# An attention layer with a rotation: sums of the partial contexts moved to the final stage, and the mask penalty of the last 192 key columns moved to TensorE

## What is computed

```
emb = silu(sin_emb(timestep)) @ W_ada + b_ada; scale, shift = split(emb)
x = ln(src) * (1 + scale) + shift
q, k, v = heads(x @ Wq + bq), heads(x @ Wk + bk), heads(x @ Wv + bv)
scores = q @ k.T / sqrt(32) + attention_bias          # the bias is B x 16 x 2048 x 2048 f32, 537 MB
scores = where(mask, -inf, scores)                    # one mask for all heads
ctx = merge_heads(softmax(scores) @ v)
x = x + (ctx @ Wo + bo); h = ln(x) * g2 + beta2
x = x + gelu2(h @ W1 + b1) @ W2 + b2
out = rotation by theta and phi of each four neighbouring columns of x
```

## Time and profile before

| | before |
|---|---|
| median of 3 runs | 3860.55 us |
| the profiled execution, its own time | 3858.61 us |
| its span, first to last instruction | 3857.0 us |
| attention stage, first bias load to last store | 510 to 2719 us |
| final stage | 2719 to 3857 us |
| granted TensorE clock, mean | 0.965 |

### The profile page before, as it was taken

One profiled execution on the slowest core, in us unless ns is written; L12 is line 12 of the kernel. 1 busy time (PEld: TensorE's weight loads), 2 busy tenths in 40 slices (PEclk: granted clock), 3 DMA queues, 4 the chain that ended last, 5 costly groups with the idle time before them and its releaser, 6 DMA issues. The chain is left out here.

```text
span 3857.0 us, 64984 instructions
## 1 busy us (share of the span) xinstructions
PE 3589.8 (93%) x18848; PEld 2074.9 (54%) x18848; DVE 2561.2 (66%) x4882; ACT 1899.6 (49%) x2483; POOL 2165.7 (56%) x595
## 2 busy tenths in 40 slices
PE   6778769999999999999999999999699999999997
PEld 2334336666666666666666666666344444444443
DVE  3444449999989999899999899999322323232232
ACT  1221227777777777777777777777211111111110
POOL 0000059999989999999999999999000000000000
PEclk8889879999999999999999999999799999999999
DMA  5556489999999999999999999997511101101000
GB/s 188 169 173 201 147 288 319 315 313 312 319 348 317 316 312 312 337 331 313 317 315 313 341 319 314 317 313 271 155 22 33 22 11 33 22 22 22 11 11 11
DMA packets 327444, 822.20 MB, mean 213 GB/s; under 512 B 165376, under 2 KB 181760, under 8 KB 250624
## 3 DMA queue, kind: packets, MB, share of 16 engines
q1 hardware_dynamic: 277376, 746.44, 57.6%
q10 hardware_dynamic: 45312, 58.74, 5.6%
q0 software_dynamic: 4736, 16.78, 1.2%
HBM read 737.95 MB, written 83.89 MB: 213 GB/s over the span
## 5 line engine op out<-in xcount | busy, mean ns | idle before, releaser
L450 POOL TENSOR_TENSOR ring<-ring,penb 128x2048 f32<-128x2048 f32 x512 | 2089.4, 4119 | 599.6 <-DMA penb<-pen_scratch 542.5
L555 ACT ACTIVATE ring<-ring,neg_max 128x2048 f32<-128x2048 f32 x512 | 1029.1, 2010 | 515.4 <-DVE neg_max L520 515.4
L618 PEld LDWEIGHTS b_T<-ident,ring 128*128 128x128 f32 x8192 | 886.7, 141 | 623.5 <-ACT probT L564 427.6
L618 PE MATMUL b_T<-ident,ring 128*128 128x128 f32 x8192 | 1158.7, 281 | 1.9 <-DVE probT L492 1.3
L492 DVE COPY probT<-b_T 128x512 f32<-128x512 f32 x1024 | 668.0, 684 | 70.5 <-PE b_T L618 70.5
L506 DVE CUSTOM_DVE_ANT_0 ring<-scores,ring,max_part 128x1024 f32<-128x1024 f32 x512 | 657.6, 1284 | 74.2
L506 DVE CUSTOM_DVE_ANT_0 ring<-scores,ring 128x1024 f32<-128x1024 f32 x512 | 622.2, 1215 | 43.6 <-PE scores L601 43.6
L601 PE MATMUL scores<-keys,queries 128*128 (+1 forms) x2048 | 606.5, 418 | 46.6 <-DMA queries<-q_parts 45.4
L781 POOL TENSOR_TENSOR y_out<-rot_a,rot_b 128x512 f32<-128x512 f32 x32 | 50.3, 1572 | 1020.8 <-DVE rot_b L890 1020.0
L564 ACT COPY probT<-b_T 128x512 f32<-128x512 f32 x1024 | 542.8, 580 | 30.2 <-PE b_T L618 24.0
L634 PE MATMUL bank_ctx<-probT,values 128*32 128x512 f32 x4096 | 546.8, 607 | 0.0
(11 more groups left out here) (91 smaller groups left out, 1926.1 us busy)
## 6 DMA issues: line engine op xcount, KB each, us to landing
ring<-in_fside_Bx16xSxS SPq DMA_DIRECT2D x512, 1024.0 KB, 5.8
keys<-k_parts SPq DMA_DIRECT2D x256, 256.0 KB, 6.8
values<-v_heads ACTq DMA_DIRECT2D x128, 256.0 KB, 6.0
queries<-q_parts SPq DMA_DIRECT2D x512, 64.0 KB, 6.8
pen_scratch<-pen SPq DMA_DIRECT2D x8, 2048.0 KB, 7.2
penb<-pen_scratch SPq DMA_DIRECT2D x32, 512.0 KB, 12.3
xin<-in_x ACTq DMA_DIRECT2D x8, 1024.0 KB, 5.2
mask_in<-in_mask_Bx1xSxS_bk ACTq DMA_DIRECT2D x8, 1024.0 KB, 7.3
```

What stands on the lines that cost most here:

```text
L450: nc.gpsimd.tensor_tensor(ring[:, j, :], ring[:, j, :], penb[:, j, :], ALU.add).then_inc(masked, 1)
L555: nc.scalar.activation(ring[:, k, :], ring[:, k, :], ACT.Exp, bias=neg_max[:, k:k + 1], accum_out=sums[:, k:k + 1]).then_inc(exp_done, 1)
L618: last = nc.tensor.transpose(bankT[n % 2][:, c * P:(c + 1) * P], ring[:, slot, at:at + P], ident[:])
```

## The change

In the attention stage `close`, `sel4`, `bank_sum`, the reciprocal and the scaling go. The four partial contexts are copied (L571 as before) and stored unsummed: 256 KB for 4 tiles in place of 64 KB. The freed PSUM bank becomes a third transpose bank. GpSimd adds the penalty to columns 0 to 1855 only; for the last 192 TensorE adds a matmul of a bf16 identity with `penb` to the last score matmul's bank. VectorE computes the negated sum with a running minimum, so the separate negation L520 goes, and it places one `copy_quarter` behind each `add` (quarter 3 with a lag of three tiles). TensorE's waits stand one or two matmuls ahead of where they are needed. ScalarE keeps row sums and minima of all trips in SBUF and copies the 8 minima once in a trip.

In the final stage SyncE loads the partial contexts, 4 x 256 KB for each block of four heads (c = 0 to 3 of a unit), into two buffers. GpSimd sums them with two additions (of 1024 and 512 columns); TensorE transposes the broadcast reciprocals in place of the context; VectorE multiplies the two. All other fronts are one f later. The rotations of unit u-1 (`late`) are spread over f = 0 to 3 of unit u, behind `hidden`. W1 and W2 are loaded by ScalarE's queue, Wo after the first two context blocks.

```diff
 # phase_b, GpSimd and TensorE
-  nc.gpsimd.tensor_tensor(ring[:, j, :], ring[:, j, :], penb[:, j, :], ALU.add)
+  nc.gpsimd.tensor_tensor(ring[:, j, 0:POOL_MASKED], ring[:, j, 0:POOL_MASKED], penb[:, j, 0:POOL_MASKED], ALU.add)
+                if live(i, NT):
+                    if c == CH - 1:
+                        pe.wait_ge(pen_in[j], (it // H) * 16 + 16)
+                        last = nc.tensor.matmul(scores[c][:, CW - PE_MASKED:CW], identb[:], penb[:, j, POOL_MASKED:S],
+                                                start=False, stop=True)
+            def free_before_turn(it, j, c):
+                t = it * R + j - 2
+                if live(t, NT):
+                    if c == 0:
+                        pe.wait_ge(exp_done, t + 1)
+                    else:
+                        need(pe, out_dve, t * 2 - 1)
-                if j % QT == 2:
-                    close(it, j)
 # phase_b, VectorE
                 add(it, j, 0)
+                copy_quarter(it, j, 3, 3)
                 add(it, j, 1)
-                    nc.vector.tensor_scalar(neg_max[:, j:j + 1], max_part[:, j, CH - 1:CH], -2.0, 0.5, ALU.mult, ALU.mult)
-                copy_quarter(it, j, 2)
-                copy_quarter(it, j, 3)
+                copy_quarter(it, j, 2, 2)
 # phase_b, ScalarE
-                      ctx_out[:, hh, :, :].rearrange("p t d -> p (t d)")).then_inc(ctx_stored[hh], 16)
+                                  ctxp[:]).then_inc(ctx_stored, 16)
 # phase_c, SyncE
+                for c in range(DB):
+                    if isinstance(v, int) and c == 2:
+                        load_vectors()
+                    need(sp, ctxT_ready, v * DB + c - 1)
+                    for k in range(4):
+                        sp.dma_start(parts[DH * k:DH * (k + 1), c % 2, :, :],
+                                     ctx_scratch[bass.ds(v * H + 4 * c + k, 1)].rearrange("o (g d) q -> d (o g) q", d=DH)).then_inc(part_ld[c % 2], 16)
 # phase_c, GpSimd
+            def add_parts(v, c):
+                pool.wait_ge(part_ld[c % 2], v * 128 + (c // 2) * 64 + 64)
+                nc.gpsimd.tensor_tensor(parts[:, c % 2, 0:2, :], parts[:, c % 2, 0:2, :], parts[:, c % 2, 2:4, :], ALU.add).then_inc(halved, 1)
+                pool.wait_ge(halved, added_by_pool(v, c))
+                nc.gpsimd.tensor_tensor(parts[:, c % 2, 0, :], parts[:, c % 2, 0, :], parts[:, c % 2, 1, :], ALU.add).then_inc(summed, 1)
+            def between(v):
+                add_parts(v, 0)
+                add_parts(v, 1)
+                finish(v - 2, 0)
+                finish(v - 2, 1)
+                add_parts(v, 2)
+                finish(v - 2, 2)
+                add_parts(v, 3)
+                finish(v - 2, 3)
 # phase_c, the order of VectorE
             with eng.Fori(1, NU - 1) as u:
                 for f in range(FB + 2):
                     ffn(u, f)
+                    front(u + 1, f)
+                    late(u - 1, f)
```

More of the change, by code:

```diff
@@ L439, in _ @@
                         load_head(b, pair, h, False)
-            for i in range(2):
-                sp.wait_ge(ctx_stored[i], 16 + TRIPS * 16)
+            sp.wait_ge(ctx_stored, UNITS * 16 + 16)
         @block.gpsimd
@@ L621, in weigh @@
-            def weigh(it, j):
-                n = (j - 2) % QT
-                unit = it * 2 - 2 if j < 2 else it * 2 - 1 if j < 6 else it * 2
-                hh = 1 if 2 <= j < 6 else 0
-                if live(unit, UNITS):
-                    if n == 0:
-                        pe.wait_ge(v_in[hh], it * 16 if j == 2 else it * 16 + 16)
-                        need(pe, ctx_copied, unit)
-                    pe.wait_ge(out_act if n < 2 else out_dve, (unit * QT + QT - 1) * 2 + n % 2 + 1)
-                    for c in range(4):
+                if n == 2 and live(t, NT):
+                    need(pe, out_dve, t * 2)
@@ new lines, in turn @@
+                for c in range(QR):
+                    if c == 2:
+                        if n == 0 and live(t, NT):
+                            need(pe, out_act, t * 2)
+                        if n == 1:
+                            copied_before_weigh(it, j)
+                        if n == 2 and live(t, NT):
+                            pe.wait_ge(out_act, t * 2 + 1)
+                    if live(t, NT):
+                        at = (QR * n + c) * P
+                        last = nc.tensor.transpose(turn_bank(slot, n)[:, c * P:(c + 1) * P], ring[:, slot, at:at + P], ident[:])
@@ new lines, in turn, with weighed, copied_before_weigh @@
+                if live(t, NT):
+                    last.then_inc(turned, 1)
+            def weighed(it, j):
+                unit = it * 2 - 2 if j < 2 else it * 2 - 1 if j < 6 else it * 2
+                return (j - 2) % QT, unit, 1 if 2 <= j < 6 else 0
+            def copied_before_weigh(it, j):
+                n, unit, hh = weighed(it, j)
+                if live(unit, UNITS):
+                    pe.wait_ge(out_act if n < 2 else out_dve, (unit * QT + QT - 1) * 2 + n % 2 + 1)
+            def weigh(it, j):
+                n, unit, hh = weighed(it, j)
+                if live(unit, UNITS) and n == 0:
+                    pe.wait_ge(v_in[hh], it * 16 if j == 2 else it * 16 + 16)
+                    need(pe, ctx_copied, unit)
+                for c in range(4):
+                    if live(unit, UNITS):
@@ L634, in weigh @@
                         last = nc.tensor.matmul(bank_ctx[DH * c:DH * (c + 1), :], values[:, hh, QR * n + c, :],
                                                 probT[:, hh, QR * n + c, :], start=(n == 0), stop=(n == 3))
-                    if n == 3:
-                        last.then_inc(pv_done, 1)
-            def close(it, j):
-                unit = closing(it, j)
-                if live(unit, UNITS):
-                    pe.wait_ge(ctx_copied, unit + 1)
-                    pe.wait_ge(ctx_normed, unit + 1)
-                    for t in range(QT):
-                        last = nc.tensor.matmul(bank_sum[:, t * DH:(t + 1) * DH], ctxp[:, t * P:(t + 1) * P], sel4[:],
-                                                start=True, stop=True)
-                    last.then_inc(ctx_summed, 1)
+                if live(unit, UNITS) and n == 3:
+                    last.then_inc(pv_done, 1)
@@ L703, in phase_c @@
         consts_ready = sem("consts_ready")
-        ctx_ld, xm_ld = sem("ctx_ld"), sem("xm_ld")
-        ctx_turned = sem("ctx_turned")
+        part_ld, xm_ld = [sem(f"part_ld{i}") for i in range(2)], sem("xm_ld")
+        halved = sem("halved")
+        summed = sem("summed")
+        first_summed = sem("first_summed")
+        recip_ready = sem("recip_ready")
+        wide_ready = sem("wide_ready")
+        recip_turned = sem("recip_turned")
         ctxT_ready = sem("ctxT_ready")
@@ new lines, in finish @@
+            def finish(u, t):
+                pool.wait_ge(rotated, u * QT + t + 1)
+                need(pool, y_stored[t % 2], u * 32 + (t // 2) * 16)
+                nc.gpsimd.tensor_tensor(y_out[:, t % 2, :], rot_a[:, t % 2, :], rot_b[:, t % 2, :], ALU.add).then_inc(y_ready, 1)
+                pool.wait_ge(y_ready, u * QT + t + 3)
+                pool.dma_start(out[bass.ds(u, 1), t * P:(t + 1) * P, :].rearrange("o p n -> (o p) n"),
+                               y_out[:, t % 2, :]).then_inc(y_stored[t % 2], 16)
@@ new lines, in _ @@
+            add_parts(0, 0)
+            add_parts(0, 2)
+            for c in range(DB):
+                add_parts(1, c)
+            def between(v):
[7 more added lines that the diff above has]
+                finish(v - 2, 3)
+            between(2)
+            with pool.Fori(3, NU) as v:
+                between(v)
@@ L789, in _ @@
+            for u in (NU - 2, NU - 1):
+                for t in range(QT):
+                    finish(u, t)
             for i in range(2):
```

339 lines of the change are left out of this document (170 added, 169 removed).

## The result

The changed kernel takes 3949.84 us (median of four executions, 3944.27 to 3977.22; a fifth took 3931.72) against 3860.34 for the kernel before: ratio 1.0234, 95% interval 1.0182 to 1.0286. A gain to 3680 was forecast; it is a loss of 2.3%. The profiled execution is the longest of its runs, 3977.22 us with a span of 3975.4.

The account below looks back on a forecast made before the run. TensorE and VectorE, tied together, were taken to set the 33.65 us trip, with GpSimd and DMA close behind, DMA becoming first limit. 3857 - 133 (attention) - 45 (final stage) = 3679 us of span, given as 3680; forecast 3640 to 3730, range 3590 to 3775.

Parts of the forecast that it names:

- a store is issued one step earlier: Attention, ScalarE: the earlier store is covered by its slack, busy 25.8 of 33.65 us; uncovered, 0.3 us a trip.
- if the new copy of the context costs the queues more than its bytes: Stated condition for being wrong: the larger context copy costs the DMA queues more than its bytes; no size given.
- SyncE's wait for the slot has room: Attention, bias tile loads: 8 slots of 3.9 us against some 20 us for a tile's load through transposes.
- The DMA term: Attention: 11.28 MB a trip takes 30.7 to 32.9 us; with 0.8 for lockstep, 31.5, saving 133 us.
- GpSimd 3.74: Attention: GpSimd's penalty addition over 1856 of 2048 columns falls from 4.108 to 3.74 us a tile.
- The mask matmul: Attention, TensorE: the new 192-column mask matmul costs 0.11 us a tile, between 0 and 0.25.
- TensorE's tile: Attention: 3.5 to 4.05 us, taken as 3.75, or 30.0 a trip; earlier waits could remove gaps between groups.
- The stall at the change of unit: Final stage: spreading the rotations removes TensorE's 8.4 us stall, 0.5 left for safety, saving 55 us over seven changes.
- GpSimd's sums: Final stage: summing partial contexts takes 15 to 30 us of a 127 us unit, hidden in pauses.
- The start: Start of the final stage, 55.0 us before: 10 us longer from the added loads, between -5 and +20.
- (d): Rival: waits for transfers lower TensorE's clock to a mean of 0.84; trip 35.7 us, about 3943 us; chance 0.06.
- (b): Rival: DMA keeps today's busy rate or TensorE its gaps; trip 32.4 to 32.9 us, about 3753 us; chance 0.22.

Follow-up runs that it names:

- e17: The changed kernel with ScalarE's store of the context issued one step later, where it stood before the change; 3766.1 us.
- e1: The changed kernel with SyncE issuing the query loads one tile earlier in its queue; 3831.1 us.
- e11: The changed kernel with the query loads issued from ScalarE's queue instead of SyncE's; 3873.7 us.
- e6: e1 without the low-by-low product of q and k: three key loads instead of four, six query loads instead of eight; 3714.7 us.
- e16: The changed kernel with the first 512 columns of a tile's scores matmul done twice, slowing TensorE; 3918.2 us.
- e9: e1 with e5's single values load, e6's three key parts, and W1 and W2 loads issued behind unit 0's four reciprocal copies; 3700.9 us.
- e12: The changed kernel with ScalarE issuing the W1 and W2 loads behind unit 0's four reciprocal copies, not ahead of them; 3930.0 us.
- e5: e1 with a head's values loaded once in a trip and the second buffer copied by ScalarE; 3803.6 us.
- e7: e1 with keys loaded only for the first head of each group of 16, wrong keys for the rest, timing only; 3701.2 us.

## Why the prediction was wrong, step by step

**The failed step** is the one on ScalarE's store: "a store is issued one step earlier", costed by ScalarE's own time and covered by its slack. No run showed a cost of it on ScalarE; the cost lay in what the store meets in the DMA engines. e17 puts it at 184 us, more than the whole distance between the changed kernel and the kernel before: with that one issue moved back the kernel takes 3766 us and is a gain again. Of the conditions for being wrong one named it, "if the new copy of the context costs the queues more than its bytes", but no rival carried it.

**"SyncE's wait for the slot has room"** held for the bias tiles as far as it matters (GpSimd waits 222.5 us for them in after, but VectorE for GpSimd only 4.9) and was not asked of the queries, the load with the least room in the same queue: 11.7 us before (issued 1338.06, wanted 1349.74) and 10.8 now. e1 and e11 show that much of the loss passes through here (119 and 76 us back).

**The DMA term.** The bytes were right: e17 moves 342 GB/s at a share of 0.99, and 33.0 x 342 is 11.3 MB, forecast 11.28. The rate was not: 368 GB/s was taken from stretches in which penalty tiles, large loads over all partitions, filled the queue. Between 1200 and 1600 us the best of all runs is 341 and 342, in e6 and e17, just under the 343 from which the upper end, 32.9 us a trip, was worked out. So with the store in its old place a trip is 33.0, not 31.5. The 358 GB/s of the Trainium skill (DMA: Bandwidth & Descriptors, Specifications) was not reached in these windows either.

**The engines.** GpSimd 3.74: right. The mask matmul 0.10 for 0.11: right. TensorE's tile 3.94 for 3.75: the waits set earlier took nothing out of the gaps between the groups: scores 1.02, mask 0.10, turn 0.96, weigh 1.00 and turn 0.85 make 3.93. By that alone the trip could not come under 31.5, the very time that was forecast with 0.8 us of loss already in it.

**The final stage.** The stall at the change of unit is gone, as said; 1.7 us of 8.4 are left, most of it in ScalarE's reciprocal copies (TensorE waits 1.28 us for one, at 2952.94), against 0.5 taken: 7 x 6.7 = 47 us gained for 55. GpSimd's sums hide. The start was mis-sized, +31 for +10: the forecast counted bytes on two queues, but not that ScalarE is held while it issues 8 MB. -47 and +31 are the -16 measured.

**The rivals.** (d) gave the side and nearly the number, 3943, but by luck: it needed a mean clock of 0.84, and measured were 0.94 to 0.96. The clock fell after TensorE's waits for queries and explains one slow tile of 5.4 us a trip (5.43 - 3.94 = 1.5 us); the waits themselves, 131.6 us in 1500, weigh more, some 3.2 us a trip. (b), 3753 with transfers at today's rate, is close to what e17 gives, 3766, and for the reason that it named.

**What stays open.** Why the keys' trough is so much worse when the large store goes ahead of them is seen in the slices and not taken apart; why more TensorE work (e16) gives 32 us back is not explained by it; the small store at the old step of the changed kernel, which would isolate the step, has not been run, nor has e9 with the store at its old step.

## What to carry to other kernels

Moving a DMA's issue is a change to every transfer in flight with it: cost it by what it is now beside, and look at the rate in slices of 1 us at that place, not only at the issuing engine's time. In a queue shared by loads of different urgency, compute the room of the one with the shortest, for it waits behind all the others. And take the rate of a full queue from a stretch with the same mix of shapes.

## What was unexpected in the hardware

Loads into 32 partitions at a time held the engines at nine tenths busy at 131 to 238 GB/s, where most slices before and behind them, with loads over 128 partitions, were at 380 to 430. The same 8 MB of weight loads, eight issues, held ScalarE for 16.0 us in after (4.54 and 11.48), and for 31.3 (2.92 and 28.34) in e12, where they were issued beside the loads of the second pair of context blocks; why it is twice as long wasn't taken apart. A share of 1 doesn't say how much is moved: e5 shows 1.01 at 313 GB/s and e6 1.00 at 341, and e9 0.99 and e7 0.93 with the same trip of 31.9 us.
